# Moving a router's small operations and a token count inside the attention batches of a fused attention and mixture-of-experts kernel

## The reference

```python
def _L0_xattn_ref(Q, K, V, Wq, bq, Wk, bk, Wv, bv, We, be):     # D 256, 16 heads of 16, 64 keys
    q = (Q @ Wq + bq).reshape(B, L, H, E)
    k = (K @ Wk + bk).reshape(B, S, H, E)
    v = (V @ Wv + bv).reshape(B, S, H, E)
    scores = jnp.einsum('blhe,bshe->bhls', q, k)
    A = jax.nn.softmax(scale * scores, axis=-1)
    out = jnp.einsum('bhls,bshd->blhd', A, v).reshape(B, L, H * E)
    return out @ We + be

def _L0_ffn_ref(x, router_w, router_b, expert_up, expert_down):  # 8 experts, 2 of them per token
    probs = jax.nn.softmax(x_flat @ router_w + router_b, axis=-1)
    top_w, top_idx = jax.lax.top_k(probs, TOP_K)
    comb = jnp.sum(top_w[..., None] * jax.nn.one_hot(top_idx, E), axis=1)
    for e in range(E):
        h = jax.nn.gelu(x_flat @ expert_up[e].T, approximate=False)
        output = output + comb[:, e:e + 1] * (h @ expert_down[e].T)

x = x + _L0_xattn_ref(_layernorm(x), ctx_1024, ctx_1024, ...)    # x is 4 x 512 x 256, all float32
x = x + _L0_ffn_ref(_layernorm(x), ...)
```

## Time and profile before

| | |
|---|---|
| runs | 437.22, 433.22, 435.20 us; median 435.20 |
| profiled execution | 435.32 us, of which span 433.5 us |
| mean granted TensorE clock | 0.967 of full speed |
| busy PE / DVE / ACT / POOL | 385.8 / 242.5 / 195.7 / 164.7 us |
| attention batches 1, 2, 3 (first `values` to the next) | 33.8 to 69.7, to 108.2, to 145.1 us |
| chain that ended last, by engine | PE 72%, issue 11%, DVE 6% |
| first turned rows of the second stage (L1515) | from 202.3 us |

### The profile page before, as it was taken

How to read it: one execution, slowest core, us unless ns; L and a number is a source line. 1 busy time by engine, 2 the same in 40 slices (tenths; PEclk the granted TensorE clock), 3 DMA queues, 4 the chain that set the end, 5 groups by cost and what they waited for, 6 DMA issues and landing times.

```text
span 433.5 us, 9276 instructions
## 1 busy us (share of the span) xinstructions
PE 385.8 (89%) x2205; PEld 313.7 (72%) x2206; DVE 242.5 (56%) x690; ACT 195.7 (45%) x356; POOL 164.7 (38%) x253
## 2 busy tenths in 40 slices
PE   2899888698988868988999999999999999999970
PEld 1675666466666637987788888888888888888850
DVE  3496685888788946674325574565642652323320
ACT  1365335334443422643447666484744844444420
POOL 2414220302212040015653754646565466445441
PEclk9899999999899985999999999999999999999996
DMA  8911010401121110172323783837463132232221
GB/s 270 327 49 70 28 51 0 147 2 50 49 97 48 51 50 2 48 229 68 62 40 81 188 230 57 223 88 190 121 148 48 25 49 37 37 49 35 39 37 12
DMA packets 26386, 37.19 MB, mean 86 GB/s; under 512 B 4704, under 2 KB 17440, under 8 KB 26368
## 3 DMA queue, kind: packets, MB, share of 16 engines
q1 hardware_dynamic: 19312, 26.98, 18.6%
q0 software_dynamic: 7056, 9.99, 14.6%
HBM read 27.18 MB, written 9.79 MB: 85 GB/s over the span
## 4 chain that ended last, share of the span: by engine, by line
PE 72%; issue 11%; DVE 6%; POOL 3%; ACT 3%; DMA 2%; SPq 0%; POOLq 0%; DVEq 0%; ACTq 0%
PE bankC L1545 13%; PE bankC L1205 10%; PE bankC L1207 9%; PE bankC L1206 9%; PE bankC L1546 7%; PE bankB L1523 6%; PE bankB L1205 2%; PE bankA L1515 2%; PE bankA L1295 1%; DMA bias<-bqk 1%; POOL rstd L363 1%; PE bankB L1207 1%; PE bankB L1206 1%; PE bankC L1283 1%; DVE put L948 1%
## 5 line engine op out<-in xcount | busy, mean ns | idle before, releaser
L1545 PE MATMUL bankC<-dn_w,qk_h 128*128 x256 | 94.3, 407 | 1.2 <-DVE qk_l L1140 1.2
L1546 PE MATMUL bankC<-dn_w,qk_l 128*128 x256 | 71.9, 281 | 0.0
L460 POOL DMA_INDIRECT out<-x2T,idx_s x32 | 51.5, 1610 | 18.8 <-issue 18.8
L1545 PEld LDWEIGHTS bankC<-dn_w,qk_h 128*128 128x128 f32 x256 | 48.2, 188 | 11.6 <-issue 1.4
L1205 PE MATMUL bankC<-up_w,xnT_h 128*128 (+1 forms) x128 | 53.1, 415 | 1.0 <-DVE xnT_l L1134 1.0
L1207 PE MATMUL bankC<-up_w,xnT_l 128*128 (+1 forms) x128 | 50.7, 396 | 0.0
L1206 PE MATMUL bankC<-up_w,xnT_h 128*128 (+1 forms) x128 | 50.6, 395 | 0.0
L1147 DVE SCALAR_TENSOR_TENSOR x2T<-bankC,gate,x2T 128x256 f32<-128x256 f32 x32 | 15.4, 482 | 61.8 <-ACT x2T L680 47.5
L1546 PEld LDWEIGHTS bankC<-dn_w,qk_l 128*128 128x128 f32 x256 | 48.2, 188 | 0.0
L675 ACT ACTIVATE raw<-bankC 128x512 f32<-128x512 f32 x64 | 38.4, 599 | 20.2 <-PE bankC L1207 20.2
L450 POOL DMA_INDIRECT xr<-rows,idx_g x35 | 38.5, 1100 | 20.3 <-issue 20.3
(11 more groups left out here) (255 smaller groups left out, 825.0 us busy)
## 6 DMA issues: line engine op xcount, KB each, us to landing
xall<-up SPq DMA_DIRECT2D x24, 256.0 KB
xall<-down SPq DMA_DIRECT2D x24, 256.0 KB, 4.3
rows<-xr SPq DMA_DIRECT2D x4, 528.0 KB, 3.4
raw<-up SPq DMA_DIRECT2D x4, 512.0 KB, 4.4
raw<-down SPq DMA_DIRECT2D x4, 512.0 KB, 5.1
out<-xall SPq DMA_DIRECT2D x4, 512.0 KB, 2.8
xall<-x SPq DMA_DIRECT2D x1, 1536.0 KB, 9.8
cst<-const SPq DMA_DIRECT2D x1, 640.0 KB, 8.0
```

The lines of the kernel that those rows point to most:

```text
L460: g.indirect_dma_start(out, bass.IndirectOffsetOnAxis(idx_s[:, n:n + 1], 0), y[n], None, bounds_check=T + P - 1, compute_op=ALU.add).then_ ...
L1545: mm(bankC[:, 2, :], hT_h[:, o], wd, start=(m == 0), stop=False)
L1546: last = mm(bankC[:, 2, 0:D], hT_l[:, o], wd[:, 0:D], start=False, stop=(m == KF - 1))
```

## The change

Four things change, and no computation is added or removed.

First, on PE the tiny matmuls of `positions` move from ahead of the second half of `values` and the query products to behind `den_turn`, just ahead of the first score. Second, on DVE the second low half of the turned rows goes ahead of the router's masks. (The masks become a function `chosen`.) Third, on DVE `ranks` is split: its first operation (`pk`, now `own_counts`) comes behind the low halves of the queries, and the rest, with `count`, behind `max_split`. Fourth, `scores` and `maxima` no longer run tile by tile over both halves k, but through k = 1 for the four tiles and then k = 0. The first score then waits only for the first low half of the queries, the fifth for the second. Score number 2, which overwrites the bank with the counts, waits for `own_counts`. The last change applies to all four batches, the others to batches 2 and 3.

```diff
-            def maxima(b, t):
-                for k in range(KD):
-                    n = KD * t + k
+            def maxima(b, m):
+                for n in (2 * m, 2 * m + 1):
+                    k, t = 1 - n // LT, n % LT
...
                 x_low(i, 1)
                 if with_router:
-                    ranks(i - 2, bankC[:, 2, :])
-                    count(i - 2)
+                    chosen(i - 2)
                 q_low(i)
+                if with_router:
+                    own_counts(i - 2, bankC[:, 2, :])
                 rden_split(i - 1)
...
                 max_split(i)
+                if with_router:
+                    ranks(i - 2)
+                    count(i - 2)
                 residual_norm2(i - 1)
...
-            def scores(b, t):
-
-                for k in range(KD):
-                    n = KD * t + k
+            def scores(b, m, router=False):
+
+                for n in (2 * m, 2 * m + 1):
+                    k, t = 1 - n // LT, n % LT
                     if n == 0:
+                        pe.wait_ge(v_q, KD * b + 1)
+                        pe.wait_ge(g_kbd, 4 * b + 4)
+                    if n == LT:
                         pe.wait_ge(v_q, KD * b + 2)
-                        pe.wait_ge(g_kbd, 4 * b + 4)
+                    if n == 2 and router:
+                        pe.wait_ge(v_pos, 4 * (b - 2) + 1)
...
                 x_turn(i, 1)
-                if router:
-                    pe.wait_ge(a_exp, 8 * i - 2)
-                    positions(i - 2, bankC[:, 2, :])
                 values(i - 1, range(4, 8))
                 project_q(i)
                 den_turn(i - 1)
+                if router:
+                    positions(i - 2, bankC[:, 2, :])
                 scores(i, 0)
                 rden_turn(i - 1)
-                scores(i, 1)
+                scores(i, 1, router)
```

More of the change, by code:

```diff
@@ L890, in router, with chosen @@
                     v.max_index(i8[:, t, :], v8[:, t, :], pr[:, t, :]).then_inc(v_top, 1)
+            def chosen(b):
                 dve.wait_ge(v_top, 8 * b + 8)
@@ L912, in count, with own_counts @@
                 v.tensor_copy(seen_bf[:, :], seen[:, :]).then_inc(v_seen, 1)
-            def ranks(b, counts):
+            def own_counts(b, counts):
                 dve.wait_ge(p_pos, b + 1)
@@ L919, in ranks @@
                                     .broadcast_to([P, TOPK, LT, NE]), ALU.mult).then_inc(v_pos, 1)
+            def ranks(b):
                 dve.wait_ge(v_pos, 4 * b + 1)
@@ L1015, in _ @@
             router(B - 2)
-            ranks(B - 2, bankB1)
+            chosen(B - 2)
+            own_counts(B - 2, bankB1)
+            ranks(B - 2)
             count(B - 2)
@@ L1049, in _ @@
             router(B - 1)
-            ranks(B - 1, bankB1)
+            chosen(B - 1)
+            own_counts(B - 1, bankB1)
+            ranks(B - 1)
             v.tensor_tensor(big[:, :, :], bc3(bankB1[:, LT * NE:(LT + 1) * NE], COLS - 1),
```

## The result

| | before | changed |
|---|---|---|
| median of 10 runs each | 435.45 us (433.22 to 437.22) | 429.88 us (429.01 to 433.30) |
| ratio, 95% interval | | 0.9877 (0.9854 to 0.9901) |
| profiled execution, span | 435.32, 433.5 us | 429.61, 427.8 us |
| its mean granted clock | 0.967 | 0.975 |

The changed kernel is faster by 5.6 us, where 2.5 were forecast and the range ended at 430.8. The steps that were forecast are found in the rows, but the sum was too small in two places.

A forecast was written before the change was run, and what follows sets the result against it. PE was taken to bound the kernel, busy 385.8 of 433.5 us. Batch 1 gives 0.44 us, batch 2 2.2, batch 3 -0.1, together 2.5: from 435.3 to 432.8 us, range 430.8 to 435.1.

The forecast's parts named there:

- the wait for the mask: PE's 2.08 us ahead of batch 2's counts, from masks slowed beside POOL's blocks; its removal wins 2.5 us.
- The thin cover of the masks: DVE, batches 2 and 3: masks end at 80.9, the queries' first low half is ready at 81.05; 0.15 us spare.
- The first score's wait: PE, three batches: 1.13 us goes, but only 0.44 (batch 1) or 0.27 (batches 2, 3) reaches the output projection.
- DVE's idle time among the maxima: DVE's 0.44 us of idle time among the maxima would be won three times, 1.3 us in all.
- just in time: Third score starts on PE at P + 6.1, ready near P + 7.0 (P: query products' start), when DVE finishes two maxima.
- The ranks behind the maxima: DVE, batches 2 and 3: ranks take 2.2 us, mostly hidden in idle time; iteration ends 0.3 us later against query products.
- The sign that was named: Expected in the profile after: PE waiting for `put` by 0.3 us or more.
- The 0.2 us of the counts in batch 3: PE, batch 3: query products come 0.21 us earlier because the counts no longer stand ahead of them.
- The clock at nothing in the sum: The forecast sum held no gain from TensorE's clock; a lost half-speed stretch appeared only as a rival.
- a rival with a chance of 0.15: Early batch 3: the half-speed stretch at 108 us doesn't happen, 1.4 us more gone, 431.4 us; chance 0.15.
- the case that had a chance of 0.08: Whole kernel: the changed version is faster by over 1%, 4.4 us; chance 0.08.
- The slower rival: Clock falls at `rden_turn`'s 0.6 us wait in three batches, 1.8 us each; 2.9 us slower, 438.2; chance 0.05.

The follow-up runs named there:

- e8b: Changed kernel with the router's masks ahead of the second low half again, counts still behind den_turn; mean 432.78 us, 433.7 at equal clock.
- e2: Kernel before with only the fourth part, scores and maxima bank by bank; mean 432.60 us, 433.1 at equal clock.
- e3: Changed kernel without its fourth part, scores and maxima tile by tile as before; mean 432.34 us, 432.2 at equal clock.
- e6b: Changed kernel with six dummy matmuls between the first transposes and the first query products; mean 430.17 us, 431.0 at equal clock.
- e7b: Changed kernel with the first half of att_low on GpSimd in place of VectorE; mean 429.35 us, 430.4 at equal clock.
- e9: Changed kernel with att_low's first half on GpSimd in batches 1 to 3, plus dummy matmuls at the start; 428.67 us, ratio 0.9834.
- e4: Changed kernel with all of ranks and count ahead of the reciprocals instead of behind the maxima; mean 435.29 us, 435.2 at equal clock.

## Why the prediction was wrong, point by point

1. **Where the wait for the mask came from, and that it goes: right.** The masks run at 1 us each beside POOL's blocks; the counts behind the query products and the low half ahead of the masks win 2.4 us (2.5 forecast). e8b undoes the low half's move and loses 2.4. The low half ahead of the masks with the counts in their old place was not tried; that it wouldn't do is argued from the rows, by which PE would wait for the mask there as before.
2. **The thin cover of the masks, 0.15 us: held**, with 0.34 us. The text had three masks end at POOL's boundaries; only the first two did.
3. **The first score's wait is mostly not won: right.** 1.13 us go and 0.72 come back at `rden_turn` (0.6 forecast); e2 and e3 put the banks at 1.7 and 0.9 us around the forecast 1.3. In batch 2 the output projection starts 12.29 us behind the query products in place of 12.58, 0.29 earlier (0.27 forecast), but not in the way that the text had it, and the close agreement is in part luck. DVE's idle time among the maxima did not vanish: 0.32 us of 0.44 stayed, because the third score was not there "just in time" (three such waits were 1.3 us, now 0.9). The rest came from the first two maxima, which stood closer together.
4. **The ranks behind the maxima: mis-sized.** The text took 2.2 us for them, 0.3 more than DVE's idle time would hold. They took 1.84 (90.65 to 92.49), without the 0.44 us wait that they had had in the earlier trace rows; `pk` cost nothing that can be seen, since the maxima had waited for PE by about as much. The end of the iteration came 0.2 us earlier against the query products, not 0.3 later. In batch 3 it is the same 0.2 us (26.51 to 26.28). Twice 0.5 us, less the 0.2 of point 5 and the 0.1 by which point 1 fell short, makes the 3.2 us of the rows out of the 2.5 forecast. The sign that was named, a wait of 0.3 us or more for `put`, did not come: 0.16 and 0.15 us.
5. **The 0.2 us of the counts in batch 3: wrong.** From turn to products batch 3 of the changed kernel takes 2.68 us (110.14 to 112.82) without the counts, and it took 2.68 with them. They had cost nothing there.
6. **The clock at nothing in the sum, and a rival with a chance of 0.15: the step that failed most.** The text saw that its own execution had lost 1.4 us at 108 us and asked only whether that fall would go. It priced the wait of 2.08 us by its length, since its one execution had no fall behind it, though two of three of before have one, at 1.4 us. The changed kernel's mean clock is 0.004 higher, 1.2 ± 0.9 us; in the ten timings of the result it is 0.006 above the mean of before, 1.7 us. With 3.5 for the schedule that gives 5.2, and the means of the ten and ten, 435.5 and 430.2, differ by 5.3. So of the 2.8 us that were missing, 1.0 was the schedule (0.8 of it in points 4 and 5) and some 1.7 the clock; the medians add 0.3. The cause of the clock's share stays open: the removed wait for the mask could give about 1.0 of it, but e2 and e8b have as high a clock and keep the wait. The result, 1.2% faster, is the case that had a chance of 0.08.
7. **The slower rival**, a fall at `rden_turn`: in none of nine profiled executions with 0.7 or 0.8 us of waiting there (the changed kernel four times, e2, e6b, e7b, e8b, e9). In e4, with 2.66 us there, it came, at 85 to 89 us. That is one execution.

## What to carry to other kernels

A wait of TensorE amid dense work can have two prices, its length and the clock behind it (here 2.08 us, and 1.4 more in five of seven executions), and one profiled execution shows the second only by luck: read several, and the mean clock of many timings, before a wait is priced. Compare kernels at equal mean clock; ten timings by themselves gave 5.6 us where the schedule gives 3.5. When a wait is taken away, ask which chain stands behind it; here 0.7 of 1.1 us came back one step later, and the small operations that had been in the way were only free in the place where their engine was idle. Beside GpSimd's blocks a small operation with two SBUF inputs took 0.93 to 1.08 us in place of 0.2, and the low half, which reads PSUM, kept its 0.69: put the second kind there, not the first.

## What the hardware showed that was not expected

Behind a wait of 2.1 to 2.3 us in batch 2 the clock was at 1.2 GHz in five of seven profiled executions, and in none of eleven without the wait. Eight dummy matmuls in it made a kernel faster by 2.4 to 2.6 us, from 435.3 on the same chip (435.6 over all timings) to 432.9, without moving any useful one. Behind the waits of 0.7 to 1.1 us in batch 2 (at the first score, at `rden_turn`, at the output projection) no execution has a fall; only e4's wait of 2.66 us there has one. With six dummies in PE's wait of 1.4 us at the start, e6b and e9 have no stretch at 15 us, while the changed kernel and e7b have it in four of five executions; but e3, e4 and e8b, without dummies, lack it too, so this is open. What brings the stretches at 104 to 112 us and, in e9, at 136 and 146 us was not tried.
